# Forming five of six weight products inside the layers before them, instead of all six ahead of the first layer

## The reference, cut to what matters

```python
x = x + 0.5 * stack(layernorm(x))       # stack 0
x = x + retention(layernorm(x))
x = x + 0.5 * stack(layernorm(x))       # stack 1

def stack(x):
    for i in range(6):
        x = attn_layer(shift_tokens(x), Wqkv[i], q_scale[i], k_scale[i], Wo[i]) + x
        x = ffn_layer(shift_tokens(x), ln_g[i], ln_b[i], W1[i], b1[i], W2[i], b2[i]) + x
    return x
```

## Time and profile before

| | before |
|---|---|
| time, median of 3 runs | 3583.01 us (3582.12 to 3585.25) |
| the profiled execution's own time | 3582.17 us |
| its span, first to last instruction | 3580.4 us |
| PE busy | 3406.9 us, 95% of the span |
| DVE busy | 2839.3 us, 79% |
| ACT busy | 2383.7 us, 67% |
| POOL busy | 2334.5 us, 65% |
| mean granted clock of PE (1 is 2.4 GHz) | 0.974 |

### The profile page before, as it was taken

How to read it: one execution, slowest core, us unless ns; L and a number is a source line. 1 busy time by engine, 2 the same in 40 slices (tenths; PEclk the granted TensorE clock), 3 DMA queues, 4 the chain that set the end, 5 groups by cost and what they waited for, 6 DMA issues and landing times.

```text
span 3580.4 us, 123150 instructions
## 1 busy us (share of the span) xinstructions
PE 3406.9 (95%) x51660; PEld 1859.3 (52%) x51660; DVE 2839.3 (79%) x6042; ACT 2383.7 (67%) x4153; POOL 2334.5 (65%) x2187
## 2 busy tenths in 40 slices
PE   3799999999999999999797999999999999999997
PEld 2355555555555555555363555555555555555553
DVE  1788888888888888888367888888888888888883
ACT  1566776776776776776524667767777767767764
POOL 0677766767766766767046767777777767777761
PEclk7799999999999999999898999999999999999998
DMA  5000000000000000000100000000000000000000
GB/s 192 9 11 27 23 12 27 23 12 27 22 13 27 22 13 27 21 13 4 56 1 9 10 28 21 12 28 21 12 29 21 12 28 21 12 28 22 12 5 13
DMA packets 50087, 82.93 MB, mean 23 GB/s; under 512 B 7168, under 2 KB 37120, under 8 KB 47232
## 3 DMA queue, kind: packets, MB, share of 16 engines
q1 hardware_dynamic: 49536, 75.05, 6.6%
HBM read 67.69 MB, written 7.34 MB: 21 GB/s over the span
## 4 chain that ended last, share of the span: by engine, by line
PE 91%; DVE 3%; issue 2%; ACT 1%; DMA 1%; POOL 1%; SPq 0%; DVEq 0%; POOLq 0%; ACTq 0%
PE VS L886 20%; PE QA L826 18%; PE TB L845 10%; PE TB L910 9%; PE VS L936 7%; PE TB L869 6%; PE FB L962 4%; PE FB L963 3%; PE FB L971 3%; PE VS L920 2%; PE TB L853 1%; PE FB L952 1%; PE FB L947 1%; DMA KT<-in_w_out 1%; DVE T L602 1%
## 5 line engine op out<-in xcount | busy, mean ns | idle before, releaser
L330 POOL TENSOR_TENSOR QN<-T 128x512 f32<-128x512 f32 x768 | 980.5, 1277 | 574.4 <-DVE T L602 574.4
L337 POOL TENSOR_TENSOR QN<-QN,RR 128x512 f32<-128x512 f32 x768 | 800.9, 1043 | 295.1 <-DVE RR L623 295.1
L826 PE MATMUL QA<-WQ,Y 128*128 128x512 f32 x1536 | 796.6, 617 | 23.1 <-DVE T L602 12.0
L886 PE MATMUL VS<-MW,Y 128*32 128x512 f32 x6144 | 741.9, 601 | 5.8 <-DVE Z L675 5.8
L442 ACT ACTIVATE SQ<-QA 128x512 f32<-128x512 f32 x768 | 458.9, 597 | 269.9 <-PE QA L826 259.0
L602 DVE TENSOR_TENSOR T<-QA,TAB 128x256 f32<-128x256 f32 x1536 | 569.5, 411 | 0.0
L597 DVE TENSOR_TENSOR T<-QA,TAB 128x512 f32<-128x512 f32 x768 | 512.8, 668 | 30.6 <-ACT SQ L442 16.1
L462 ACT ACTIVATE V<-VS 128x512 f32<-128x512 f32 x768 | 461.0, 600 | 96.0 <-PE VS L886 95.4
L910 PEld LDWEIGHTS TB<-CST,QN 128*128 128x128 f32 x3072 | 374.3, 142 | 256.7 <-issue 189.1
L610 DVE TENSOR_REDUCE SSQ<-SQ 128x8 f32<-128x512 f32 x768 | 486.4, 674 | 0.0
L629 DVE TENSOR_TENSOR Y<-TB,Y 64x128 f32<-64x128 f32 x384 | 111.1, 289 | 461.8 <-PE TB L853 459.2
(11 more groups left out here) (172 smaller groups left out, 4269.7 us busy)
## 6 DMA issues: line engine op xcount, KB each, us to landing
TAB<-in_tables SPq DMA_DIRECT2D x192, 128.0 KB, 2.1
WQ<-in_w_qk SPq DMA_DIRECT2D x48, 256.0 KB, 2.9
MW<-m_dram SPq DMA_DIRECT2D x12, 1024.0 KB, 4.8
m_dram<-QN SPq DMA_DIRECT2D x6, 1024.0 KB, 4.9
W1R<-in_w SPq DMA_DIRECT2D x12, 341.0 KB, 3.1
KT<-in_w_vt SPq DMA_DIRECT2D x6, 512.0 KB, 5.8
KT<-in_w_out SPq DMA_DIRECT2D x6, 512.0 KB, 6.6
W<-in_w SPq DMA_DIRECT2D x12, 192.0 KB, 2.4
```

Source lines behind the costliest of these rows:

```text
L330: po.tensor_tensor(QN[:, n % 2, k, :], T1[:, k, :], T2[:, k, :], ALU.add).then_inc(s_add, 1)
L337: po.tensor_tensor(heads(QN[:, m % 2, k, :]), heads(QN[:, m % 2, k, :]), RR[:, m % 2, 8 * k:8 * k + 8].unsqueeze(2).to_broadcast([P, 8, DH ...
L826: mm(QA[:, k % 2, :], Y[:, j * P:(j + 1) * P], WQ[:, k, :], start=True, stop=True).then_inc(s_qk, 1)
L886: last = mm(VS[32 * q:32 * q + 32, w % 2, :], Y[:, a:a + WIN], MW[:, q, :], start=True, stop=True, tile_position=(0, 32 * q), skip_group_c ...
```

## The change

Only the product of layer 0 is still formed ahead of stack 0, and it is copied straight into MW. Those of layers 1 to 5 are formed inside stack 0, four pieces of four matmuls a layer: layer l's in slots 16(l-1)+4, +8, +12 and 16l, so twenty pieces in slots 4, 8, ..., 80. A piece goes to the first 256 columns of both banks of FB, behind out_transpose and ahead of project_qk(1); DVE copies it to MW behind rotate(1). MW has two buffers, so stack 0 reads its value weights where DVE put them. SP writes each finished product to m_dram in slot 16l+2 and loads the next layer's w_vt and w_out there (WS is now a tile of its own, with one buffer). Stack 1 loads MW from m_dram, one layer ahead. On ACT the preload stands ahead of everything, and once more ahead of the second layer norm.

```diff
-        MW = sb("MW", [P, 4, 512])
+        MW = sb("MW", [P, 2, 4, 512])
+        WS = sb("WS", [P, 2, INNER])
...
+        def fold_piece(c, s):
+            if s or c % 4 or not 4 <= c < 4 + 4 * CH // 2 * (DEPTH - 1):
+                return None
+            return (c - 4) // TPL + 1, (c - 4) // 4 % 4
...
             def fold_in(l):
-                if l >= 2:
-                    sp.wait_ge(s_mm, l - 1)
+                if l == 1:
+                    sp.wait_ge(s_mm, 1)
+                elif l >= 2:
+                    sp.wait_ge(s_mp, 4 * (l - 1))
... # SP's slot
+                if s == 0 and c % TPL == 2 and c < TILES:
+                    fold_out(c // TPL)
+                    if 1 <= c // TPL < DEPTH - 1:
+                        fold_in(c // TPL + 1)
+                if s == 1 and c % TPL == 4 and c // TPL + 1 < DEPTH:
+                    if c // TPL:
+                        sp.wait_ge(s_vp, 4 * (TILES + c // TPL * TPL))
+                    v_weights(c // TPL + 1)
-                if (c - 4) % TPL == TPL - 1:
-                    sp.wait_ge(s_vp, by_tile(4, n - 4, it, 4))
-                    v_weights(nxt)
... # SP's stack()
                 if s == 0:
-                    for l in range(DEPTH):
-                        if l >= 1:
-                            fold_in(l)
-                        fold_out(l)
-                    sp.wait_ge(s_ms[0], 16)
-                v_weights(first)
+                    fold_in(1)
+                else:
+                    sp.wait_ge(s_ms[0], 16 * 3)
+                    sp.wait_ge(s_ms[1], 16 * 3)
+                    v_weights(0)
... # ACT
                 ac.wait_ge(s_lnd, 4 * NG * s + 2 * NG)
-                ac.preload_act_table_set("natural_log_exp_and_others")
...
             ac.wait_ge(s_cst, 5)
-            for l in range(DEPTH):
...
+            ac.preload_act_table_set("natural_log_exp_and_others")
+            ac.wait_ge(s_mm, 1)
+            for hq in range(2):
+                nc.scalar.activation(MW[:, 0, :, hq * P:(hq + 1) * P],
...
             stack(0)
+            ac.preload_act_table_set("natural_log_exp_and_others")
             ln_act(ac, 1)
... # DVE's slot, behind rotate(0), rotate(1)
+                if fold_piece(c, s):
+                    l, p = fold_piece(c, s)
+                    ve.wait_ge(s_mp, 4 * (l - 1) + p + 1)
+                    if l >= 2:
+                        ve.wait_ge(s_ms[l % 2], 16 * (l // 2))
+                        ve.wait_ge(s_vp, 4 * TPL * (l - 1))
+                    nc.vector.tensor_copy(
+                        MW[:, l % 2, 2 * (p % 2):2 * (p % 2) + 2, :].rearrange("p q (e c n) -> p e c q n", e=2, c=2)
+                        [:, :, p // 2, :, :], FB[:, :, 0:2 * P].rearrange("p e (q n) -> p e q n", q=2)).then_inc(s_mo, 1)
... # PE
                     if j == 0 and w == 0:
-                        pe.wait_ge(s_mw, by_layer(16, m // TPL, it, 16))
+                        if s:
+                            pe.wait_ge(s_mw, 16 * (l + 1))
+                        elif l:
+                            pe.wait_ge(s_mo, 4 * l)
... # ffn_centre
+                    if fold_piece(c, s):
+                        pe.wait_ge(s_mo, (c - 4) // 4 + 1)
...
+                def fold_weights(l, p):
+                    if p == 0:
+                        pe.wait_ge(s_ws, 32 * (l + 1))
+                    if c >= 12:
+                        pe.wait_ge(s_y, NG + (c - 12) // 4 + 1)
+                    if c % TPL == 8:
+                        pe.wait_ge(s_prb, c // TPL + 1)
+                        pe.wait_ge(s_mo, (c - 4) // 4)
+                    for ch in (2 * p, 2 * p + 1):
+                        for e in range(2):
+                            r = slice(64 * e, 64 * e + 64)
+                            at = ch % 2 * P
+                            last = mm(FB[:, e, at:at + P], WS[r, 0, ch * P:(ch + 1) * P], WS[r, 1, ch * P:(ch + 1) * P],
+                                      start=True, stop=True, tile_position=(64 * e, 0), skip_group_check=True)
+                    last.then_inc(s_mp, 1)
...
             pe.wait_ge(s_xt, 4)
-            pe.wait_ge(s_mea, 2 * DEPTH)
-            pe.wait_ge(s_med, 2 * DEPTH)
+            pe.wait_ge(s_mea, 2)
+            pe.wait_ge(s_med, 2)
             stack(0)
```

More of the change, by code:

```diff
@@ L148, in build_macaron @@
         s_mm, s_mea, s_med = sem("s_mm"), sem("s_mea"), sem("s_med")
+        s_mp, s_mo = sem("s_mp"), sem("s_mo")
         s_lmu, s_lxc, s_lsq, s_lvar = sem("s_lmu"), sem("s_lxc"), sem("s_lsq"), sem("s_lvar")
@@ L209, in fold_in @@
             def fold_in(l):
[L210 to L218 removed]
+                if l == 1:
+                    sp.wait_ge(s_mm, 1)
+                elif l >= 2:
+                    sp.wait_ge(s_mp, 4 * (l - 1))
+                sp.dma_start(WS[:, 0, :], w_vt[l]).then_inc(s_ws, 16)
+                sp.dma_start(WS[:, 1, :], w_out[l]).then_inc(s_ws, 16)
+            def fold_out(l):
+                if l == 0:
+                    sp.wait_ge(s_mea, 2)
+                    sp.wait_ge(s_med, 2)
+                else:
+                    sp.wait_ge(s_mo, 4 * l)
+                sp.dma_start(m_dram[l], MW[:, l % 2, :, :].rearrange("p a n -> p (a n)")).then_inc(s_ms[l % 2], 16)
             def down_weights(at):
@@ L729, in _ @@
                 nc.vector.tensor_copy(X[:, b * GT:(b + 1) * GT], pa(b)).then_inc(s_xt, 1)
-            for l in range(DEPTH):
-                bank = pb if l % 2 == 0 else pa
-                ve.wait_ge(s_mm, l + 1)
-                if l >= 2:
-                    ve.wait_ge(s_ms[l % 2], 16 * (l // 2))
-                for hq in range(2, 4):
-                    nc.vector.tensor_copy(QN[:, l % 2, :, hq * P:(hq + 1) * P],
-                                          bank(hq).rearrange("p (a n) -> p a n", n=P)).then_inc(s_med, 1)
+            ve.wait_ge(s_mm, 1)
+            for hq in range(2, 4):
+                nc.vector.tensor_copy(MW[:, 0, :, hq * P:(hq + 1) * P],
+                                      pb(hq).rearrange("p (a n) -> p a n", n=P)).then_inc(s_med, 1)
             stack(0)
@@ L885, in project_v @@
                     for q in range(4):
-                        last = mm(VS[32 * q:32 * q + 32, w % 2, :], Y[:, a:a + WIN], MW[:, q, :], start=True,
+                        last = mm(VS[32 * q:32 * q + 32, w % 2, :], Y[:, a:a + WIN], MW[:, l % 2, q, :], start=True,
                                   stop=True, tile_position=(0, 32 * q), skip_group_check=True)
@@ L1046, in _ @@
             last.then_inc(s_xt_ps, 1)
-            for l in range(DEPTH):
-                bank = pb if l % 2 == 0 else pa
-                pe.wait_ge(s_ws[l % 2], 32 * (l // 2 + 1))
-                if l == 1:
-                    pe.wait_ge(s_xt, 4)
-                if l >= 2:
-                    pe.wait_ge(s_mea, 2 * (l - 1))
-                    pe.wait_ge(s_med, 2 * (l - 1))
-                for ch in range(CH):
-                    for e in range(2):
-                        r = slice(64 * e, 64 * e + 64)
-                        last = mm(bank(2 * e + ch // 4)[:, (ch % 4) * P:(ch % 4 + 1) * P],
-                                  WS[r, l % 2, 0, ch * P:(ch + 1) * P], WS[r, l % 2, 1, ch * P:(ch + 1) * P],
-                                  start=True, stop=True, tile_position=(64 * e, 0), skip_group_check=True)
-                last.then_inc(s_mm, 1)
+            pe.wait_ge(s_ws, 32)
+            for ch in range(CH):
+                for e in range(2):
+                    r = slice(64 * e, 64 * e + 64)
+                    last = mm(pb(2 * e + ch // 4)[:, (ch % 4) * P:(ch % 4 + 1) * P],
+                              WS[r, 0, ch * P:(ch + 1) * P], WS[r, 1, ch * P:(ch + 1) * P],
+                              start=True, stop=True, tile_position=(64 * e, 0), skip_group_check=True)
+            last.then_inc(s_mm, 1)
             pe.wait_ge(s_xt, 4)
-            pe.wait_ge(s_mea, 2 * DEPTH)
-            pe.wait_ge(s_med, 2 * DEPTH)
+            pe.wait_ge(s_mea, 2)
+            pe.wait_ge(s_med, 2)
             stack(0)
```

29 lines of the change are left out of this document (10 added, 19 removed).

## The result

The changed kernel took 3530.82 us in the median of four runs (3529.27 to 3533.10), the kernel before beside it 3584.13 us (four runs, 3582.12 to 3591.12): a ratio of 0.9852, with a 95% interval from 0.9839 to 0.9866. That is faster by 53 us. 3530.8 lies inside the range of 3515 to 3537, but 7.8 above the predicted 3523, and outside the forecast's own range of 3518 to 3529.

What follows compares the result with a forecast made beforehand. PE was taken to bound the middle of a stack, but not the start. From 3582.2 us, 72.5 gained at the start, 1.6 paid in slot 4, 11.4 for nineteen pieces and 0.8 for the median gave 3523; range 3515 to 3537.

Steps and rivals of the forecast that it cites:

- The start: Before slot 0's first product: one weight product instead of six and no table loads in the layer norm, 72.5 us gained.
- The rival of a long layer norm: First layer norm stays at 21.64 us because of the clock or a late load: 9 us more, 3532.5; chance 0.05.
- Slot 4: While the pipeline fills and DVE bounds, the first piece (about 0.95) and DVE's copy (0.69) cost 1.6 us.
- PE's pieces: Nineteen pieces on PE at 0.6 us each, streaming 0.44 plus changes of tiling, cost 11.4 us.
- the upper bound of 0.8: Price of a piece in us if the larger tiling change is paid twice and a first weight load too.
- The estimate from a short drain: A piece priced from a drain of some 128 cycles, 0.05 us: 0.54 each, 10.3 us for nineteen.
- The copies on DVE: DVE's copies outside slot 4, 0.69 us each, fit rooms of 0.81 and 0.77 us and cost nothing.
- The rival of the copy on the path: DVE's copy waits for POOL and reaches the path: 13.3 us more for nineteen pieces, 3537; chance 0.13.
- Streaming alone: Rival: a piece on PE costs only its streaming, 0.44 us, 8.4 for nineteen: 3520.5 us; chance 0.15.
- The waits: PE's piece waits for DVE's L688, done 1.0 us early; SP's new waits delay nothing: no cost.
- The slower rival: PE's pieces wait for DVE's L688; 3.6 us each cancels the gain, 4 us gives about 3591; chance 0.02.
- The sum: Whole kernel: 3582.2 - 72.5 + 1.6 + 11.4 = 3522.7, with 0.8 for the median 3523.5, said as 3523 us.

Runs made afterwards that it cites:

- the kernel with the loads alone: Kernel before with only ACT's table choice moved ahead of the layer norm and its copies, six products still in the start: 3570.6 us, ratio 0.9964.
- the full array: Changed kernel with each piece formed by two matmuls of 128 rows instead of four of 64, no change of tiling: 3511.72 us, one run.
- the piece first: Changed kernel with the piece ahead of out_transpose instead of behind it: 3524.99 us, one run.
- the larger pieces: Changed kernel with ten pieces of eight matmuls instead of twenty of four, DVE copying 1,024 elements a partition: 3521.37 us in one run, later 3519.9 in four.
- the doubled ones: Changed kernel with the four matmuls of each piece issued twice, same result: 3529.96 us, one run.

## Why the prediction was right or wrong

**The start: right.** Predicted -72.5, measured -73.2. The 0.7 beyond it is the layer norm's start at 15.80 instead of 16.46, since PE's product and its copies ended 0.65 earlier than in the trace of before. That is chance: the repeated trace of the changed kernel has it at 16.38. The layer norm took 12.65, predicted 12.67, and the kernel with the loads alone shows that nothing else had made it long. The rival of a long layer norm falls.

**Slot 4: not told apart.** 1.4 measured, 1.6 predicted, but the filling varies by more: from slot 0's first product to the bias step of slot 7 three traces of kernels whose slots are those of before took 112.8 to 114.5, the changed kernel 116.0 and 114.8, and the run without pieces 119.9. The agreement is luck as far as these traces go.

**PE's pieces: the step that failed.** "I take 0.6, between both sizes paid once and little more" was mis-sized: a piece measured 0.83 to 0.84, past even the upper bound of 0.8. At that price nineteen cost 15.8 and not 11.4. The rows of the value projection and of the scores show a change of tiling as seen from one side, the delay until the next group's first start, 0.15 and 0.09. Entering the piece cost just such a delay, 0.09. What was left out is what comes behind: 0.21 until project_qk may start and 0.10 within it. In before project_qk's weights were loaded 0.16 us ahead of its matmul, at 957.71; behind a piece that load starts only with it:

```profile
957.71 0.36 PEld L826 LDWEIGHTS QA<-WQ,Y 128*128 128x128 f32 x2
```

```profile
898.32 0.30 PEld L838 LDWEIGHTS QA<-WQ,Y 128*128 128x128 f32 x2
```

The Trainium skill says in TensorEngine Tiling (Array Packing), Key Properties, that a change of the tiling mode drains the engine. The runs agree with it: 0.39 a piece go with both changes (the full array), 0.19 with one (the piece first). The estimate from a short drain, 0.54 a piece, was too low by 0.3.

**The copies on DVE: right.** 0.681 us each, free by the run without them. The rival of the copy on the path falls, and with it the one case of the range that lay above. It holds for the copy of 512 elements alone; the one of 1,024 used the room up. By SBUF — State Buffer in the Trainium skill (Who interferes with whom) a DVE instruction with at most one input from SBUF does not contend with POOL outside the two-port modes. The twenty copies from PSUM at 681 to 682 ns, nineteen of them beside a POOL instruction all along, agree.

**Streaming alone: wrong for this kernel,** and exactly right (0.44) for the one whose tiling doesn't change.

**The waits: right.** No piece waited for DVE. In both traces PE's transposes waited for POOL for about 30 us in all (35 times after, 45 before), and the value projection for DVE 5.0 and 5.8 us. The slower rival falls with this.

**The sum.** With 0.83 for 0.6 the forecast would be 3523.5 + 19 x 0.23 = 3527.9. Of the remaining 2.9 to the measured median, the start gave back 0.7, so 3.6 are due to something that the sum has no term for: the trace of before from which it was made had the shortest slots 8 to 72 of stack 1 of thirteen.

That was visible only in part beforehand: PE stands still for 0.3 to 2.8 us within or ahead of some groups with no releaser in the trace. In stack 1 of the changed kernel the chain of waits has this row (start, us, what):

```profile
1935.95 1.99 issue
```

Such stops are in every trace, and they are tied to a place in the program. PE behind a stop in slot 62 of stack 0 and behind the stop of that row, first in the changed kernel and then in its repeated trace:

```profile
1077.59 0.38 PE L952 MATMUL VS<-KT,QT 64*32 64x64 f32 x18 [0.42 <-issue]
...
1937.94 0.33 PE L952 MATMUL VS<-KT,QT 64*32 64x64 f32 x10 [1.99 <-issue]
```

```profile
1077.73 0.38 PE L952 MATMUL VS<-KT,QT 64*32 64x64 f32 x18 [0.42 <-issue]
...
1936.63 0.33 PE L952 MATMUL VS<-KT,QT 64*32 64x64 f32 x10 [2.54 <-issue]
```

Each stands ahead of the same matmul in both traces. For a count, take as a stop what the distance from one matmul's start to the next has over its usual length at that place of a slot, if that is over 0.25 us and no releaser is shown. In slots 8 to 72 of stack 0 the changed kernel then has 14 stops in one trace and 15 in the other, and 12 of them are the same. Number PE's matmuls in the order of the trace: from one stop of a stack to the next it is 126 or a multiple of it, within three. Of 317 such stops in slots 8 to 87 of both stacks, in thirteen traces, one falls outside this. Most such places show no stop, and how long one is differs from run to run. So where PE can stop is a matter of the program, and a change that adds or takes matmuls moves these places. What PE does there no trace shows.

The stops close the account. In slots 8 to 72 of stack 0 they add up to 8.3 and 8.7 us in the two traces of the changed kernel, 6.0 and 5.0 in those of before, 6.3 and 4.5 with the larger pieces and 3.5 with the doubled ones. Take them off, and the pieces at the price of their pair (0.83; 0.64 put first; 0.44 on the full array; 1.28 doubled; 1.39 and, put first, 1.20 for the larger ones), and all thirteen traces leave 1069.6 to 1071.1 us. In stack 1 the stops are 7.7 us in the first trace of the changed kernel and 2.9 in that of before, which is the table's 4.9. And from slot 8 of stack 0 to the end they come to 37.3 us in the repeated trace of the changed kernel and 29.0 in that of the larger pieces beside it: with the 2.7 of the tiling 11.0 us, where these two executions differ by 9.4. The run on the full array has 26.1, the changed kernel's first trace 41.7; with 20 x 0.39 = 7.8 for the tiling that is 23.4, and the two executions, 3511.72 and 3533.10, lie 21.4 apart. That is an account and not a test: no run moved the stops alone.

## What to carry to other kernels

Filler work on PE between other matmuls costs more than its streaming when it uses another tiling of the array: here 0.40 us for the way in and out, beside 0.44 of work. Put such pieces where the tiling changes anyway, or make fewer and larger ones, but not both without a look at the engine that copies the result: here a copy of twice the size used up its room. Read the price from the start of the group two steps on, not from the start of the next one. Before moving a wait off the start, look at what else stands in it: one moved choice of ACT's tables gave 9 us by itself.

When two profiles are to be compared over a long stretch, take a stretch with the same instructions in both as the yardstick; here it differed by up to 5 us in 1075, so that a price of 0.2 us a piece could be read only from pairs of slots, and from several, since one pair can hold a stop of PE. Ask of such a stop whether it stands ahead of the same instruction in a second trace, before it is called noise.

## What the runs showed of the hardware

- A change from the full array to tiles of 64 x 128 and back costs PE 0.09 us in, 0.21 out, and 0.10 in the group behind it. It is not hidden by the weight load, which starts later than without it (with the matmul instead of 0.16 us ahead).
- Eight table loads of 1.28 us each cost the path 9.0 us, 1.1 each.
- DVE's copies of 512 elements a partition from PSUM take 0.68 us with POOL idle and with POOL busy alike.
- PE's stops with no visible releaser, of 0.25 to 1.5 us in slots 8 to 87, follow one another at multiples of 126 matmul records (within three) in 316 of 317 cases. They add up differently from program to program and from run to run: the same 64 slots took 1074.5 to 1079.4 us.
